# The first (conditioning) stage of a two-layer LoRA and SwiGLU kernel, put into one order for all token tiles

## The reference

```python
# L0_cond: a base product, and a LoRA term with the adapter of each sequence
base_out = jnp.einsum('bti,oi->bto', x, W) + b
A = lora_As[adapter_mapping]                    # 512 x 16 for each sequence
Bm = lora_Bs[adapter_mapping]                   # 16 x 512
lora_h = jnp.einsum('bti,bir->btr', x, A)
c = base_out + jnp.einsum('btr,bro->bto', lora_h, Bm) * 2.0
# L0_ffn: (silu(c @ W_gate.T) * (c @ W_up.T)) @ W_down.T, then x = x + that
```

## Time and profile before

| what | value |
|---|---|
| median of 3 runs | 1023.51 us (1022.88 to 1025.2) |
| the profiled execution's own time | 1018.27 us |
| its span, first to last instruction | 1016.5 us |
| mean granted TensorE clock | 0.998 |
| PE busy | 1000.7 us |
| DVE, ACT, POOL busy | 566.8, 413.0, 191.1 us |

### The profile page before, as it was taken

The page is one execution under the profiler, slowest core; times in us unless marked ns, Lnnn a source line. Parts: engine busy times, 40 slices in busy tenths (PEclk is TensorE's granted clock), DMA queues, the critical chain, the costliest instruction groups (busy, mean ns, idle before and its releaser), DMA issues.

```text
span 1016.5 us, 13762 instructions
## 1 busy us (share of the span) xinstructions
PE 1000.7 (98%) x4795; PEld 836.0 (82%) x4795; DVE 566.8 (56%) x979; ACT 413.0 (41%) x780; POOL 191.1 (19%) x172
## 2 busy tenths in 40 slices
PE   8899999999999999999999999999999999999998
PEld 6888887888888888888888888888878688888886
DVE  4655466887784323585332497233295267666662
ACT  3655466555661333572333473333353132322210
POOL 3332022563400131400113220111350000000000
PEclk9999999999999999999999999999999999999999
DMA  9698767766877766877766877866696302222211
GB/s 327 225 345 292 239 209 279 259 248 236 284 274 247 204 191 195 274 236 255 234 191 195 244 228 247 278 191 196 193 358 227 124 1 84 94 84 89 88 42 63
DMA packets 111403, 210.17 MB, mean 207 GB/s; under 512 B 12260, under 2 KB 12260, under 8 KB 111080
## 3 DMA queue, kind: packets, MB, share of 16 engines
q1 hardware_dynamic: 108800, 200.88, 60.0%
q0 software_dynamic: 2400, 8.41, 2.5%
q10 hardware_dynamic: 136, 0.01, 0.0%
HBM read 154.20 MB, written 55.05 MB: 206 GB/s over the span
## 4 chain that ended last, share of the span: by engine, by line
PE 87%; DVE 7%; DMA 3%; issue 1%; SPq 1%; ACT 1%; POOL 0%; DVEq 0%; ACTq 0%; POOLq 0%
PE bank L1402 86%; DVE cop_lo L1108 2%; DVE op_lo L1122 2%; DMA wring<-wd_scratch 1%; DMA c<-c_scratch 1%; PE bank L1565 1%; PE bank L1426 1%; DMA ab<-in_ab_table,row_i 1%; DMA w_raw<-in_w 0%; DMA wg_raw<-in_w_gate 0%; DVE xa_lo L1051 0%; DVE wring L1091 0%; DVE c_t L1104 0%; DVE c L1113 0%; DVE c L1106 0%
## 5 line engine op out<-in xcount | busy, mean ns | idle before, releaser
L1402 PE MATMUL bank<-cop_hi,wring 128*128 128x512 f32 x1234 | 381.4, 390 | 2.2 <-ACT bank L838 2.2
L1402 PEld LDWEIGHTS bank<-cop_hi,wring 128*128 128x128 f32 x1234 | 231.8, 188 | 51.1 <-ACT bank L838 3.1
L1402 PE MATMUL bank<-cop_lo,wring 128*128 128x512 f32 x616 | 239.9, 389 | 0.0
L1402 PE MATMUL bank<-op_hi,wring 128*128 128x512 f32 x560 | 174.3, 390 | 0.5 <-DMA wring<-wd_scratch 0.5
L1136 DVE TENSOR_TENSOR v<-bank,p7s 128x512 f32<-128x512 f32 x44 | 30.4, 692 | 196.9 <-PE bank L1402 196.9
L1402 PEld LDWEIGHTS bank<-cop_lo,wring 128*128 128x128 f32 x616 | 115.7, 188 | 23.9
L1402 PEld LDWEIGHTS bank<-op_hi,wring 128*128 128x128 f32 x560 | 105.2, 188 | 23.0 <-DMA wring<-wd_scratch 0.9
L1402 PE MATMUL bank<-op_lo,wring 128*128 128x512 f32 x280 | 109.1, 390 | 0.0
L661 POOL TENSOR_TENSOR h_t<-h,h 128x512 f32<-128x512 f32 x20 | 26.3, 1314 | 383.9 <-DVE h L1155 383.9
L1122 DVE TENSOR_TENSOR op_lo<-h,op_hi 128x512 fp32r<-128x512 f32 x100 | 73.5, 755 | 5.5 <-ACT op_hi L828 5.5
L869 ACT ACTIVATE s<-bank 128x512 f32<-128x512 f32 x44 | 26.3, 598 | 122.4 <-PE bank L1402 122.4
(11 more groups left out here) (177 smaller groups left out, 1701.8 us busy)
## 6 DMA issues: line engine op xcount, KB each, us to landing
wring<-wgu_scratch SPq DMA_DIRECT2D x231, 256.0 KB, 2.9
wring<-wd_scratch SPq DMA_DIRECT2D x140, 256.0 KB, 4.7
wgu_scratch<-wring SPq DMA_DIRECT2D x77, 256.0 KB, 2.4
x_raw<-in_x SPq DMA_DIRECT2D x32, 256.0 KB, 4.7
c_scratch<-c_out SPq DMA_DIRECT2D x32, 256.0 KB, 4.3
c<-c_scratch SPq DMA_DIRECT2D x32, 256.0 KB, 4.3
raw<-x_scratch SPq DMA_DIRECT2D x32, 256.0 KB, 4.1
out<-res SPq DMA_DIRECT2D x32, 256.0 KB, 2.0
```

The lines of the kernel that those rows point to most:

```text
L1402: return e.matmul(out_ap, lhs, rhs, start=start, stop=stop, skip_group_check=True)
```

## The change

What it does, engine by engine:

- PE: turn_a(0) goes ahead of chunk 2 and lora_in(0) ahead of chunk 3 of tile 0's base products. In tiles 1 to 7 the base products of bank 0 come first, then turn_a(t), base of bank 1, lora_in(t), base of banks 2 and 3, and only then the four closing products in a row.
- ACT and DVE: at the head of tile t: turn_a(t), split_x(t+1), lora_in(t) (in tile 0 split_x(1) is first); then the four points m with close_c and the spread work. In turn_a the two a parts come before the two b parts.
- DVE: row_i is computed ahead of the first split. POOL: gather(t+1) is issued at m = 0 of tile t, and no gather stands before the loop but gather(0).
- c_out has four buffers and semaphores in place of two; h_masked moves to another place in SBUF. The order of uses of the ring banks follows.

```diff
-    c_out = [work(f"c_out{s}", [TOK], F32) for s in range(2)]
-    h_masked = work("h_masked", [TOK], F32)
+    c_out = [work(f"c_out{m}", [TOK], F32) for m in range(KC)]
...
-    c_ring = [("a", 0, g, "dve") for g in range(NG)] + [("h", 0, 0, "dve")]
-    c_ring += [("a", 1, g, "dve") for g in range(NG)]
+    c_ring = []
     for t in range(NT):
...
+        c_ring += [("a", t, g, "dve") for g in range(NG)] + [("h", t, 0, "dve")]
...
-            for o_ in range(2):
-                e.wait_ge(c_stored[o_], DMA * 2 * (2 * s + 2))
+            for m in range(KC):
+                e.wait_ge(c_stored[m], DMA * (2 * s + 2))
...
-        gather(1)
-        gather(2)

         for t in range(NT):
             for m in range(KC):
-                if m == 0 and 0 < t < NT - 2:
-                    gather(t + 2)
+                if m == 0 and t + 1 < NT:
+                    gather(t + 1)
...
                              ACT.Copy).then_inc(a_hi_done, 1)
+            for g in range(NG):
                 e.wait_ge(ab_in[g], DMA * (t + 1))
...
         def close_c(t, m):
             e.wait_ge(pe_acc, nth(t, m))
-            n = 2 * t + m // 2
-            if n > 0:
-                e.wait_ge(c_stored[m % 2], DMA * n)
+            if t > 0:
+                e.wait_ge(c_stored[m], DMA * t)
...
# ACT
         split_x(0)
-        turn_a(0)
-        e.wait_ge(small_in, 3 * DMA)
-        lora_in(0)
-        turn_a(1)
         for t in range(NT):
-            if t + 1 < NT:
+            if t == 0:
+                split_x(1)
+            turn_a(t)
+            if 0 < t < NT - 1:
                 split_x(t + 1)
+            lora_in(t)
+            if t == 0:
+                e.wait_ge(small_in, 3 * DMA)
+                e.wait_ge(w0_lo_done, KC)
             for m in range(KC):
-                if (t, m) == (0, 0):
-                    e.wait_ge(w0_lo_done, KC)
                 close_c(t, m)
-                if m == 0 and 0 < t < NT - 1:
-                    turn_a(t + 1)
-                if m == 1 and t + 1 < NT:
-                    lora_in(t + 1)
                 for n in d_due(t, m):
                     down_hi(n)
...
# DVE
         e.wait_ge(dve_chain, links[0])
+        e.wait_ge(slots_in, DMA)
+        e.tensor_scalar(row_i[:, :], slot_i[:, :], float(R), r_f[:, 0:1], ALU.mult, ALU.add).then_inc(rows_done, 1)
         split_x(0)
-        turn_a(0)
-        lora_in(0)
-        turn_a(1)
         for t in range(NT):
-            if t + 1 < NT:
+            if t == 0:
+                split_x(1)
+            turn_a(t)
+            if 0 < t < NT - 1:
                 split_x(t + 1)
+            lora_in(t)
             for m in range(KC):
-                if m == 0 and 0 < t < NT - 1:
-                    turn_a(t + 1)
-                if m == 1 and t + 1 < NT:
-                    lora_in(t + 1)
...
# PE
-            if k == KC - 1:
+            if k == 2:
                 turn_a(0)
+            if k == 3:
+                lora_in(0)
             for m in range(KC):
                 cond_base(0, m, k)
-        lora_in(0)
-        turn_a(1)
         for t in range(NT):
             for m in range(KC):
                 if t > 0:
                     e.wait_ge(c_closed, nth(t - 1, m))
                     for k in range(KC):
                         cond_base(t, m, k)
-                if m == 0:
-                    e.wait_ge(lh_lo_done, t + 1)
-                    e.wait_ge(b_lo_done, NG * (t + 1))
+                    if m == 0:
+                        turn_a(t)
+                    if m == 1:
+                        lora_in(t)
+            e.wait_ge(lh_lo_done, t + 1)
+            e.wait_ge(b_lo_done, NG * (t + 1))
+            for m in range(KC):
                 cond_lora(t, m)
-                if m == 0 and 0 < t < NT - 1:
-                    turn_a(t + 1)
-                if m == 1 and t + 1 < NT:
-                    lora_in(t + 1)
```

More of the change, by code:

```diff
@@ L104, in build @@
     xa_lo = [work(f"xa_lo{s}", [KC, TOK], F32R) for s in range(2)]
+    h_masked = work("h_masked", [TOK], F32)
     within(res_region, KC * ROW)
@@ L234, in build @@
     ab_in = [sem(f"ab_in{g}") for g in range(NG)]
-    c_stored = [sem(f"c_stored{s}") for s in range(2)]
+    c_stored = [sem(f"c_stored{m}") for m in range(KC)]
     slots_in, small_in = sem("slots_in"), sem("small_in")
@@ L287, in nth @@
         return t * KC + m + 1
-    c_ring = [("a", 0, g, "dve") for g in range(NG)] + [("h", 0, 0, "dve")]
-    c_ring += [("a", 1, g, "dve") for g in range(NG)]
+    c_ring = []
     for t in range(NT):
-        if 0 < t < NT - 1:
-            c_ring += [("a", t + 1, g, "dve") for g in range(NG)]
-        if t + 1 < NT:
-            c_ring += [("h", t + 1, 0, "dve")]
+        c_ring += [("a", t, g, "dve") for g in range(NG)] + [("h", t, 0, "dve")]
     l_ring = []
@@ L572, in sync_program @@
                 e.wait_ge(c_closed, nth(t, m))
-                e.dma_start(c_dram[t, m], c_out[m % 2][:, :]).then_inc(c_stored[m % 2], DMA)
+                e.dma_start(c_dram[t, m], c_out[m][:, :]).then_inc(c_stored[m], DMA)
                 for n in d_due(t, m):
@@ L580, in sync_program @@
                     load_c(0, m // 3)
-        for i in range(2):
-            e.wait_ge(c_stored[i], DMA * 2 * NT)
+        for m in range(KC):
+            e.wait_ge(c_stored[m], DMA * NT)
         for n in range(N_G):
@@ L768, in close_c @@
             e.wait_ge(pe_acc, nth(t, m))
-            n = 2 * t + m // 2
-            if n > 0:
-                e.wait_ge(c_stored[m % 2], DMA * n)
-            e.activation(c_out[m % 2][:, :], acc[m][:, :], ACT.Identity, bias=b0_sb[:, m:m + 1]).then_inc(c_closed, 1)
+            if t > 0:
+                e.wait_ge(c_stored[m], DMA * t)
+            e.activation(c_out[m][:, :], acc[m][:, :], ACT.Identity, bias=b0_sb[:, m:m + 1]).then_inc(c_closed, 1)
         def gate_up_hi(n):
@@ L1056, in split_x @@
                                     ALU.subtract).then_inc(w0_lo_done, 1)
[L1057 to L1060, removed]
         def turn_a(t):
```

## The result

The changed kernel takes 1027.62 us (median of 6 runs, 1025.09 to 1029.3) against 1022.7 (6 runs, 1019.51 to 1025.2) of the kernel before on the same chip: ratio 1.0058, 95% interval 1.0039 to 1.0078, so 4.0 to 8.0 us slower. The profiled execution took 1025.09 with a span of 1023.3 us, against 1018.27 and 1016.5: +6.8. TensorE's own busy time is the same (1000.8 against 1000.7), so the 6.8 us are time in which it stood still. The lower clock is inside the busy time, and it took about the same from both executions: by the granted clock 1.7 us at the start before, by the pace of the matmuls 1.7 us near 150 after.

The account below looks back on a forecast made before the run. PE was busy 1000.7 of 1016.5 us, so only its standing still or lower clock could change. -6.5 + 8.3 + 1.7 + 3.3 = +6.8 us, added to the median 1023.51, gave 1030.3; range 1026 to 1035.5.

Parts of the forecast that it names:

- Part 1: Start of the stage, tile 0: removed PE waits gain 7.0 us at most, less 0.3 and 0.2, so 6.5.
- no gather stall: Tile 0's transposes: PE's wait for gathered rows, put between 0 and 2.7 us and taken as 0.3.
- lh_lo behind POOL's sums: Before tile 0's closings: lh_lo late by 0 to 1.5 us as down_sums(0) falls beside it; 0.2 taken.
- The open question of the forecast: Gather 0: whether its packets come earlier with the 2.2 us earlier issue or still begin in 11:12.
- rival 2: Start gains little, tail still jams: PE waits 2.7 us for rows, lh_lo up to 1.5 late; 1033, chance 0.15.
- the bound of 1.5: Tile 0's lh_lo: upper bound in us of its delay from POOL's sums, read from four splits at 29.35.
- Steady tiles: Later tiles between start and tail: every operand in time at 17.60 us a tile, so a change of 0.
- Part 2: Tile 6 to 7: turn_a(7) stands behind cop work that waits for c, PE stands for a_lo(7), +8.3 us.
- The clock, +1.7: After PE's 8 us of standing in tile 7: lower clock costs 1.7 us, bounds 0 and 3.4.
- Part 3: End of the stage: second-half cop work behind close_c(7, 1) delays gate/up step 6, +3.3 us, bounds 2 to 3.6.
- Case 3: Tail stays hidden: parts 2 and 3 (13.3 us) fall under 4.5; 1021, at best 1017, chance 0.05.
- The 1.5 given there: In Case 3: cost in us of the end of the stage, within a result of -2.1 or better.

Follow-up runs that it names:

- experiment 8: experiment 6 with one POOL wait added, holding the second weight sums until b_lo of tile 7 is done: 1015.09 us, ratio 0.9932 to the kernel before.
- experiment 7: The changed kernel with POOL's down_sums(0) moved behind the second gather: one run, 1029.3 us, no interval.
- Experiment 1: The changed kernel with row_i computed behind the first two splits, where it was before: 1032.71 us, ratio 1.0103 to the kernel before.
- Experiment 2: The changed kernel with the first four loads of c issued one tile earlier: 1023.03 us, ratio 1.0023 to the kernel before.
- experiment 3: The changed kernel with turn_a(7) of ACT and DVE moved ahead of the cop work, loads of c still late: 1022.35 us, ratio 1.0009.
- experiments 4: The changed kernel with first loads of c a tile earlier and all cop work of tiles 6 and 7 ahead of their closings: 1016.56 us, ratio 0.9946.
- experiment 6: As experiments 4, but three of tile 6's seven cop steps put behind close_c(6,1): 1017.01 us, ratio 0.995 to the kernel before.
- Experiment 5: As experiments 4, but tile 7's cop work stays behind close_c(7,1) and close_c(7,2), as in the changed kernel: 1021.37 us, ratio 0.9985.

## Why the prediction was right, point by point

The direction, the mechanism and the profiled time (1025.1 forecast, 1025.09 measured) came out. The median is 2.7 under the forecast. That is not in a term of the sum: the difference was added to a median of 1023.51, the kernel before came out at 1022.7 in the 6 runs, and the two medians lie 4.9 apart where the two profiled executions lie 6.8 apart. Executions of the kernel before scatter by 5.7 us among these six (1019.51 to 1025.2), and by up to 10 in the larger sets (1017.06 to 1027.28 in 23 runs); both profiled ones were quicker than the rest of theirs. The scatter goes with the mean granted clock: of the 11 runs of the kernel before beside experiment 8, one with 0.997 had a span of 1018.7 us and one with 0.993 a span of 1026.2; of the six of the changed kernel the profiled one had 0.997, the others 0.993 to 0.995. A sum that hits one execution to 0.1 us has luck in it. The range of 1026 to 1035.5 is a little wider than its own terms, which add up to 1026.8 and 1034.8; the measured median lies in either.

- **Part 1, start, -6.5.** Closings of tile 0 start at 23.38, against 23.15 + 0.5 forecast. Taken apart: no gather stall in this execution (0.3 taken), 0.3 for lh_lo behind POOL's sums (0.2 taken; experiment 7 shows the cause), and base products that began 0.15 earlier. The open question of the forecast, whether the gather's first packets move with its issue, is answered by the trace: issued at 4.56 they begin just before 9.25, where before they were issued at 6.70 and began after 11.5. Experiment 1 shows 2.2 us of waits without the earlier index, and 1.6 of lower clock behind them, which rival 2 of the forecast had not priced. The slowed splits that it read from the kernel before (4.00 us at 29.35) are three of normal length and one of 2.15 beside POOL's sums, so the bound of 1.5 is what one instruction lost there; here it lost 0.7. But the term had scatter that I gave only to rival 2: of the eight profiles with the early index, PE waited for no gather in five (the changed kernel, 2, 3, 4, 6) and for 1.1 to 1.6 us in three (5, 7, 8). And I named no wait for a_lo(0): split_x(1) stands ahead of turn_a(0) on ACT and DVE, and where x's rows came late PE waited 0.3 to 0.6 us for a_lo (experiments 2, 3, 7, 8).
- **Steady tiles, 0.** Right: 17.605 us a tile from tile 0 to 6 and no wait of PE.
- **Part 2, +8.3.** 7.96. With T = 129.01, PE stood from T+9.4 to T+17.4 (T+9.2 to T+17.5 forecast). The loads' landing was 4.27 (4.3 forecast, from SP's row at 132.50 to c_t at 136.77), the cop chain 7.2 (7.2); POOL's sums were over at 129.9, ahead of it. Experiments 2 and 3 show both factors.
- **The clock, +1.7.** 1.7: 18 matmuls of 256 columns at 0.213 in place of 0.12. The size was taken from waits of 2.9 and 1.9 us, and that it fits one of 8.0 is luck: behind the same wait, 8.73 us in experiment 1 and 8.04 in experiment 7, the matmuls at the lower level cost 1.1 and 2.6 us.
- **Part 3, +3.3.** From the end of the closings to step 6 it was 6.6 us, against 6.5 forecast and 3.3 before. Experiment 5 shows it apart from part 2.
- **Rivals.** Case 3, the tail stays hidden, decided under 4.5 us for parts 2 and 3 together. Experiment 2 is that case made by hand: with c a tile earlier a_lo(7) is still 3.0 us late (2.9 forecast there; three steps slowed by POOL's sums, which the forecast lacked, make up for two subtractions that it counted and that ran ahead), the clock stays up, and the kernel is level with before, ratio 1.0023, not faster. The 1.5 given there to the end of the stage was too little, since its 3.3 does not hang on c's landing (experiment 5). Case 2 did not come in the profile of the changed kernel; part of it did in 5, 7 and 8.

## What to carry to other kernels

When a step is put into "the same order for all tiles", look for the tiles where other work shares the queues: the first six tiles gained or kept their time and the last two lost it, as a_lo(7) came to stand behind work that waited for a transfer. On an engine that takes nothing out of order, first issue the operand that the bounding engine wants next, then the work that can wait for memory; and issue the loads of such work a tile ahead of it (experiments 4, 6 and 8 keep the new order and win 0.5 to 0.7%). And keep GpSimd's tensor_tensor away from stretches in which VectorE is the one behind.

## What was not expected of the hardware

- **The length of a wait does not by itself decide the clock.** Behind waits of 1.92 and 2.43 (experiment 3), 2.31 (4), 2.21 (6), 3.00 (5) and 8.0 us (the changed kernel) windows of 2.5 us show a granted clock of 0.50 to 0.74; behind 2.04 (the changed kernel) and 3.01 (2) it stayed at 1.00. What differs between them, no run here tells.
- **A GpSimd tensor_tensor beside a VectorE tensor_tensor** of two SBUF operands in 32 bit makes the latter 1.03 to 1.39 us in place of 0.69, by how much of it they share. Experiments 7 and 8 took the GpSimd work away and the 0.69 came back. I had read the effect from the kernel before and priced it at 0.2 us for one instruction. In the changed kernel the seven cop steps do not meet it; with c loaded earlier they do, and 7.2 us become 11.2 (experiment 6), which the expectation of experiment 2 lacked.
- **The gather of 512 KB through loaded queues** lands with a scatter that moves PE by 0 to 1.6 us from one execution to the next.
